# An edge stage of a graph network: the one-hot of an edge's rank is made by edge and turned a batch ahead

## The reference

```
k, q, v = typed_linear(x, ntype, Wk / Wq / Wv)
kw = rel_apply(k[src], etype, Watt);  m = rel_apply(v[src], etype, Wmsg)
a  = (kw * q[dst]).sum(-1) * pri[:, etype].T / sqrt(16)
ex = exp(a - segment_max(a, dst)[dst]);  alpha = ex / segment_sum(ex, dst)[dst]
agg = segment_sum(alpha[..., None] * m, dst)
out = silu(typed_linear(agg, ntype, Wa)) * al + x * (1 - al)   # al = sigmoid(skip[ntype])
x  = layernorm(out) * g + b
```

## Time and profile before

| | us |
|---|---|
| median of 3 runs | 3420.66 (3420.48 to 3424.94) |
| span of the profiled execution | 3418.8 |
| first gather of the first edge stage | 444.8 |
| first gather of the second edge stage | 1995.0 |
| last gather of the second edge stage | 3186.2 |

### The profile page before, as it was taken

One profiled execution on the slowest core, in us unless ns is written; L12 is line 12 of the kernel. 1 busy time (PEld: TensorE's weight loads), 2 busy tenths in 40 slices (PEclk: granted clock), 3 DMA queues, 4 the chain that ended last, 5 costly groups with the idle time before them and its releaser, 6 DMA issues. The chain is left out here.

```text
span 3418.8 us, 52858 instructions
## 1 busy us (share of the span) xinstructions
PE 2097.2 (61%) x12592; PEld 1812.6 (53%) x12592; DVE 2154.3 (63%) x5522; ACT 1534.9 (45%) x5149; POOL 1947.8 (57%) x2030
## 2 busy tenths in 40 slices
PE   2567726666666666666566626666666666666565
PEld 1455515556566555655444525556655555555544
DVE  6576527666666666666555626666666666666577
ACT  0015514444444444544555614444444444444554
POOL 4415555666666666666355564666666666666265
PEclk6568867776767777677677866776777767777655
DMA  5416655555555555555245554555555555555321
GB/s 125 80 74 262 274 159 143 152 154 157 154 153 153 154 155 151 156 154 152 71 188 200 218 161 141 148 153 155 152 155 155 154 157 156 153 153 151 111 56 31
DMA packets 386069, 511.26 MB, mean 150 GB/s; under 512 B 75321, under 2 KB 298235, under 8 KB 373268
## 3 DMA queue, kind: packets, MB, share of 16 engines
q0 software_dynamic: 101952, 326.75, 30.8%
q1 hardware_dynamic: 274712, 179.39, 17.9%
q10 hardware_dynamic: 9104, 1.86, 0.3%
HBM read 382.63 MB, written 142.96 MB: 154 GB/s over the span
## 5 line engine op out<-in xcount | busy, mean ns | idle before, releaser
L1242 POOL DMA_INDIRECT g_rows<-node_kv,edge_key_sb x1564 | 1478.4, 945 | 913.1 <-issue 415.8
L1412 ACT ACTIVATE acc<-g_ps_sum 128x127 f32 x1564 | 420.5, 269 | 691.9 <-issue 498.9
L1477 PE MATMUL g_ps_sum<-g_hot,g_rows 128*128 128x128 f32 x3128 | 597.1, 348 | 163.5 <-ACT acc L1416 118.0
L1496 PE MATMUL g_ps_q<-g_qw,g_hot_t 128*128 128x128 f32 x3128 | 629.6, 372 | 106.7 <-DVE g_rows L1268 43.5
L1416 ACT ACTIVATE acc<-acc,g_gained,g_scale x1564 | 601.1, 384 | 136.0 <-issue 120.5
L1477 PEld LDWEIGHTS g_ps_sum<-g_hot,g_rows 128*128 128x128 f32 x3128 | 545.1, 259 | 203.7 <-ACT acc L1416 138.2
L1496 PEld LDWEIGHTS g_ps_q<-g_qw,g_hot_t 128*128 128x128 f32 x3128 | 586.6, 282 | 119.5 <-issue 58.0
L1522 PE MATMUL g_ps_a<-g_ends,head_of_row 112*8 112x56 f32 x224 | 38.0, 270 | 551.9 <-DVE g_alpha L1303 461.9
L1485 PE MATMUL g_ps_hot<-ident,g_hot_t 128*128 128x128 f32 x1564 | 310.9, 325 | 50.6 <-issue 29.0
L1268 DVE TENSOR_TENSOR g_rows<-g_rows,g_ps_q 128x512 f32<-128x512 f32 (+1 forms) x446 | 263.3, 608 | 118.2 <-remote 85.2
L1522 PEld LDWEIGHTS g_ps_a<-g_ends,head_of_row 112*8 112x8 f32 x224 | 13.5, 88 | 576.1 <-issue 576.1
(11 more groups left out here) (247 smaller groups left out, 3204.1 us busy)
## 6 DMA issues: line engine op xcount, KB each, us to landing
g_qw<-node_q SPq DMA_DIRECT2D x1564, 64.0 KB
g_rank_row<-edge_rank SPq DMA_DIRECT2D x110, 448.0 KB
g_rows<-node_kv,edge_key_sb POOLq DMA_INDIRECT x1564
node_agg<-n_agg SPq DMA_DIRECT2D x24, 256.0 KB, 2.3
node_rows<-node_x SPq DMA_DIRECT2D x2, 1792.0 KB
node_q<-l_blank_q SPq DMA_DIRECT2D x1, 3200.0 KB
node_q<-n_q_sb,node_slot POOLq DMA_INDIRECT x112
node_kv<-n_kv,node_id POOLq DMA_INDIRECT x112
```

The costliest lines, as they stand in the source:

```text
L1242: g_.indirect_dma_start(out=rows[b % U][:, g, :], out_offset=None, in_=scratch["kv"][:, :], in_offset=bass.IndirectOffsetOnAxis(ap=tab["ke ...
L1412: a.activation(acc[:, bass.ds(w + 1, P - 1)], ps_sum[q % 2][:, n, 1:P], ACT.Copy).then_inc(s["copied"], 1)
L1477: ins = t.matmul(ps_sum[q % 2][:, n, :], rows[b % U][:, g, D:2 * D], hot[b % U][:, g, :], start=True, stop=True)
L1496: ins = t.matmul(ps_q[q % 2][:, n, :], hot_t[b % 2][:, g, :], qw[b % 2][:, g, :], start=True, stop=True)
```

## The change

The one-hot is now made with edges on the partitions: VectorE compares a row of numbers 0 to 127 in PSUM (`place_ps`, the same in every partition) with a column of ranks that stays in SBUF for the whole kernel (`tab["rank"]`, 128 x 784 bfloat16). The result is `hot` (four buffers, `HOT`), and `sums` reads it as it is. TensorE turns it a batch ahead, in step b the tiles of batch b + 1 (`following`), and ScalarE copies the turned tiles to a single `hot_t`, which `spread` reads; a copy waits until the spread of the same group of the batch before is done, a spread until its group is copied, and the first turn of a batch until its one-hot is made. The DMA of the row of ranks, its buffer and SP's wait are gone, and with them the tail of zeros in DRAM. In the step of TensorE groups 0 and 1 of the turn stand together behind sums(old, 1), in front of the ends matmul; in ScalarE's, turned(following, 0) stands behind means(old, 1). Before the first step TensorE turns and ScalarE copies batch 0. The stage of tables turns a fourth array, the ranks, and VectorE copies it in front of the counting loop.

```diff
@@ edge_tables
+                dve.wait_ge(s["pe"], 5)
+                did(v.tensor_copy(tiles_of(tab["rank"][:, :]), ps_t[1][:, 0:K7, 0:Q]))
                 dve.wait_ge(s["lows"], 1)
...
-                for i, a in enumerate((keyf, lo, hi)):
-                    pe.wait_ge(s["dv"], (7, 7, 14)[i])
+                for i, a in enumerate((keyf, lo, hi, rank)):
+                    pe.wait_ge(s["dv"], (7, 7, 14, 14)[i])
+                    if a is rank:
+                        pe.wait_ge(s["lows"], 1)
@@ edge_stage, SP
-                    if b + 1 < BATCHES:
-                        sp.wait_ge(s["hot_t"], b + 1)
-                        ranks(b + 1)
-
-                ranks(0)
@@ edge_stage, VectorE
                 def one_hot(b):
-                    n = SIZES[b]
-                    dve.wait_ge(ranks_in[b % 2], 16 * (b // 2 + 1))
-                    if b >= 2:
-                        dve.wait_ge(s["spread"], GROUP[b - 1])
-                        dve.wait_ge(s["turned_ps"], GROUP[b - 1])
-                    v.tensor_tensor(hot_t[b % 2][:, 0:n, :].rearrange("p g e -> p (g e)"), rank_row[:, 0:n * P], number_ps.to_broadcast([P, n * P]),
-                                    ALU.is_equal).then_inc(s["hot_t"], 1)
+                    at, n = FIRST[b], SIZES[b]
+                    if b >= HOT:
+                        dve.wait_ge(s["sums"], GROUP[b - HOT + 1])
+                    v.tensor_tensor(hot[b % HOT][:, 0:n, :], place_ps.rearrange("p (o r) -> p o r", o=1).to_broadcast([P, n, P]),
+                                    tab["rank"][:, at:at + n].rearrange("p (g o) -> p g o", o=1).to_broadcast([P, n, P]),
+                                    ALU.is_equal).then_inc(s["hot"], 1)
@@ edge_stage, ScalarE
                     act.wait_ge(s["turned_ps"], q + 1)
-                    a.activation(hot[b % U][:, four[0]:four[-1] + 1, :], ps_hot[q % 2][:, 0:len(four), :], ACT.Copy).then_inc(s["turned"], 1)
+                    if b >= 1:
+                        act.wait_ge(s["spread"], GROUP[b - 1] + k + 1)
+                    a.activation(hot_t[:, four[0]:four[-1] + 1, :], ps_hot[q % 2][:, 0:len(four), :], ACT.Copy).then_inc(s["turned"], 1)
...
                     if has(old, 0):
                         means(old, 0)
-                    if has(new, 0):
-                        turned(new, 0)
                     if has(old, 1):
                         means(old, 1)
+                    if has(following, 0):
+                        turned(following, 0)
@@ edge_stage, TensorE
                     if k == 0:
                         pe.wait_ge(s["message"], b + 1)
-                        pe.wait_ge(s["turned"], GROUP[b + 1])
...
                     if has(old, 0):
                         sums(old, 0)
-                    if has(new, 0):
-                        turn(new, 0)
                     if has(new, 2):
                         spread(new, 2)
                     if has(old, 1):
                         sums(old, 1)
-                    if has(new, 1):
-                        turn(new, 1)
+                    for k in range(2):
+                        if has(following, k):
+                            turn(following, k)
```

More of the change, by code:

```diff
@@ L1157, in edge_stage @@
     q_in = [s[f"q_in{u}"] for u in range(2)]
-    ranks_in = [s[f"ranks_in{u}"] for u in range(2)]
     EARLY = 8
+    HOT = 4
     with ExitStack() as st:
@@ L1164, in edge_stage @@
         qw = [sb(f"qw{u}", [P, G, D]) for u in range(2)]
-        rank_row = sb("rank_row", [P, G * P], BF16)
-        hot_t = [sb(f"hot_t{u}", [P, G, P]) for u in range(2)]
-        hot = [sb(f"hot{j}", [P, G, P]) for j in range(U)]
+        hot_t = sb("hot_t", [P, G, P])
+        hot = [sb(f"hot{j}", [P, G, P]) for j in range(HOT)]
         score = sb("score", [P, G, H])
@@ L1432, in step @@
                     new, mid, old = in_flight(b)
+                    following = b + 1 if b + 1 < BATCHES else None
                     has = lambda batch, k: batch is not None and k < len(FOURS[batch])
@@ L1456, in step @@
                         means(old, 3)
-                    if has(new, 3):
-                        turned(new, 3)
+                    if has(following, 3):
+                        turned(following, 3)
                     if new is not None:
                         flags(new)
+                for k in range(len(FOURS[0])):
+                    turned(0, k)
                 over(step, 2)
@@ L1476, in sums @@
                     for n, g in enumerate(FOURS[b][k]):
-                        ins = t.matmul(ps_sum[q % 2][:, n, :], rows[b % U][:, g, D:2 * D], hot[b % U][:, g, :], start=True, stop=True)
+                        ins = t.matmul(ps_sum[q % 2][:, n, :], rows[b % U][:, g, D:2 * D], hot[b % HOT][:, g, :], start=True, stop=True)
                     ins.then_inc(s["sums"], 1)
@@ L1481, in turn @@
                     q = GROUP[b] + k
+                    if k == 0:
+                        pe.wait_ge(s["hot"], b + 1)
                     if q >= 2:
@@ L1484, in turn @@
                     for n, g in enumerate(FOURS[b][k]):
-                        ins = t.transpose(ps_hot[q % 2][:, n, :], hot_t[b % 2][:, g, :], c["ident"][:, :])
+                        ins = t.transpose(ps_hot[q % 2][:, n, :], hot[b % HOT][:, g, :], c["ident"][:, :])
                     ins.then_inc(s["turned_ps"], 1)
@@ L1491, in spread @@
                         pe.wait_ge(q_in[b % 2], 16 * sum(SIZES[b % 2:b + 1:2]))
-                        pe.wait_ge(s["hot_t"], b + 1)
+                    pe.wait_ge(s["turned"], q + 1)
                     if q >= 2:
@@ L1495, in spread @@
                     for n, g in enumerate(FOURS[b][k]):
-                        ins = t.matmul(ps_q[q % 2][:, n, :], hot_t[b % 2][:, g, :], qw[b % 2][:, g, :], start=True, stop=True)
+                        ins = t.matmul(ps_q[q % 2][:, n, :], hot_t[:, g, :], qw[b % 2][:, g, :], start=True, stop=True)
                     ins.then_inc(s["spread"], 1)
@@ L1527, in step @@
                         sums(old, 2)
-                    if has(new, 2):
-                        turn(new, 2)
+                    if has(following, 2):
+                        turn(following, 2)
                     if has(old, 3):
                         sums(old, 3)
-                    if has(new, 3):
-                        turn(new, 3)
+                    if has(following, 3):
+                        turn(following, 3)
                     if mid is not None:
@@ L1536, in step @@
                         t.matmul(scale_ps[:, 0:2 * SIZES[mid]], c["head_of_feature"][:, :], share[:, :, 0:SIZES[mid]], start=True, stop=True).then_inc(s["scale_ps"], 1)
+                for k in range(len(FOURS[0])):
+                    turn(0, k)
                 over(step, 2)
@@ L1561, in gnn @@
         tab["pass"] = sb("tile_pass_sb", [H, T], BF16)
+        tab["rank"] = sb("edge_rank_sb", [P, T], BF16)
         unsorted = sb("unsorted", [1, 1], I32)
```

34 lines of the change are left out of this document (15 added, 19 removed).

## The result

The changed kernel takes **3463.8 us** (3461.1 to 3467.4, four runs), the kernel before 3422.8 (3420.5 to 3427.6, four runs): a ratio of 1.0117, interval 1.0102 to 1.0132. It is 41 us slower. The forecast was 3434, slower by 13; the measured time lies in the stated range and outside the forecast's own range of 3428 to 3442, just under the price of the rival "TensorE becomes the bound" (3466 to 3540, chance 0.21).

What follows compares the result with a forecast made beforehand. GpSimd's gather stream, pausing twice for late TensorE signals, was taken to set a 21.0 us batch. Span 3418.8 + 3.2 tables + 10 starts + 106 x 0 = 3432, plus 2 to the median: 3434 us; range 3385 to 3505.

Steps and rivals of the forecast that it cites:

- TensorE becomes the bound: Rival, chance 0.21: turned group 0's copy behind means(old, 1) makes the next first sums late; 3466 to 3540 us.
- What sets the pace: Edge stages: the gather stream delays TensorE's signals and sets its own pace, 21.0 us a batch; compute engines have slack.
- its sign of being wrong: Edge stages: the prediction called itself wrong if the batch is not 21.0 us long.
- The row of ranks at nothing: Edge stages: dropping the row's 112 DMAs was taken to gain 0, with 0.24 us a batch as the other end.
- the row held the gathers: Rival, chance 0.23: without the row the pause before gather 8 shrinks 0.24 us a batch, 25 us; 3409 or 3399.
- the slack grows: Rival, chance 0.04: TensorE's clock granted in full more often, first sums' signal earlier, the 1.65 us pause goes; 3259 us.
- The one-hot at 2.0 us: VectorE's one-hot from rank column and PSUM row: 2.0 us against today's 2010 ns, cost 0.
- They fit in: cost 0: TensorE: turn groups 0 and 1, waiting for the one-hot, fit its idle time before the ends matmul; cost 0.
- turns push out the ends matmul: Rival, chance 0.04: the ends matmul's signal then comes late, 2 us a batch or more; 3640 us.
- The chain that it gave: Copy of turned group 0 delays turn 2, scale matmul 1.1 us later, then next batch's first sums; decides from 0.8 us.
- Start of each edge stage: Batch 0's turn, copy and spread come first while gathers delay signals: 5 us a stage, 10 us in all.
- Stage of tables: VectorE's copy of the ranks stands in front of the counting loop: 3.2 us, ends 1.6 and 3.2.

Runs made afterwards that it cites:

- e11: The changed kernel unaltered, run again on a chip where the kernel before takes 2809.6 us: 2810.8 us, ratio 1.0003.
- e2: Changed kernel with a DMA of a row of ranks, which nothing reads, and its two waits put back: 3463.7 us, ratio 1.0132.
- e3: Kernel before with the row of ranks loaded only for batch 0, so part of the computation is left out: 3417.1 us, ratio 0.9992.
- e1: Changed kernel with turn groups 0 and 1 placed behind the ends matmul and the transpose of alpha: 3426.9 us, ratio 1.0012.
- e4: Changed kernel with ScalarE's copy of turned group 0 put back in front of means(old, 1): 3429.5 us, ratio 1.0025.
- e5: Changed kernel with one signal behind turn 1 counting for groups 0 and 1: 2810.6 us, where the kernel before takes 2809.3 us; ratio 1.0006.
- e7: Kernel before with turn groups 0 and 1 and ScalarE's copy of group 0 moved as in the changed kernel: 2814.4 us against 2809.3, ratio 1.0015.
- e10: Kernel before with turn groups 0 and 1 and ScalarE's copy of group 0 moved, run again on another chip: 2817.9 us against 2813.4, ratio 1.0019.
- e8: Changed kernel with turn groups 0 and 1 behind the ends matmul and the tables' rank copy on ScalarE: 2806.1 us against 2809.3, ratio 0.9992.

## Why the prediction was right or wrong

**What sets the pace: right, for 80 batches of 104.** The prediction read the two pauses as TensorE's signals arriving late while gathers stream. e11 bears it out: no late signal, no pause, and a batch of 17.5 us, which is the 14 gathers alone. But its sign of being wrong was a batch that is not 21.0 us long, and 24 batches are not (21.3 to 22.6).

**The row of ranks at nothing: right.** e2 and e3. The rival that the row held the gathers, at 0.24 us a batch, is out. So is "the slack grows": the clock in the window went from 0.73 to 0.75, and both pauses stayed.

**The one-hot at 2.0 us: right**, 2012 ns, and it starts at the same 1.56 us after gather 0 as before.

**"They fit in: cost 0", for turns 0 and 1 in front of the ends matmul: this is the step that failed.** The fit itself held: turns from 3.63 us, the ends matmul over at 6.28 in the median of both kernels. But the prediction costed TensorE's time and not its signals', though its first part says that these are late while gathers stream. In TensorE's order both turns stood in front of the ends matmul before, too, but they had mostly run some 4 us earlier (TensorE idle 4.52 us there); now both wait for the one-hot, and the second ends only 0.7 to 1.6 us before the end of the ends matmul, on which VectorE's second half depends. Held batches came of it, 47 for 6, and 36 us in all where 0 was put. The rival "turns push out the ends matmul" had the right place and the chance of 0.04; its own mechanism, a matmul issued later, did not occur, and its 2 us a batch came in 24 of 104 batches and as 1.28 us.

**"TensorE becomes the bound" (0.21)** had the right price and the right sign to look for: the second pause above 2.0 us with the first sums over less than 0.5 us before it. That is what the 24 batches show (0.27 us). The chain that it gave is not what makes them. In the batches that are not held the scale matmul is at 13.8 instead of 13.1 us, 0.7 later where 1.1 was forecast, and the first sums start at 17.5 as before; and in e1, where ScalarE's copy stays behind means(old, 1), the steady batches are only 4.4 us longer in all than before. What e4 gains is in the held batches, and there the copy's place does count, beside the turns' and not by itself. That the measured time lies in the stated range is therefore luck in good part: the range went up to 3505 for this rival, and the loss came by another way.

**Start of each edge stage, 2 x 5 us: wrong, it costs 0.3 and 1.7.** The last copies of batch 0 came through within 1 us (first edge stage, changed kernel):

```profile
464.13 3.35 PE L1483 MATMUL g_ps_hot<-ident,g_hot 128*128 128x128 f32 x14 [14.41 <-DVE g_hot L1248]
...
468.43 0.38 ACT L1415 ACTIVATE g_hot_t<-g_ps_hot 128x256 f32<-128x256 f32 x1 [0.74 <-PE g_ps_hot L1483]
...
517.33 2.02 DVE L1265 TENSOR_REDUCE g_score<-g_rows 128x112 f32<-128x1792 f32 x1
```

The reduction stands 61.7 us after the first gather, 61.8 before. In the second edge stage it is 3.4 us late (63.8 against 60.4), and 1.7 of that is left after three batches.

**Stage of tables, 3.2 us: right in its size**, but the first gather is 10.9 us late in this profile. The first hots start 2.8 us later; the rest is the counting loop, whose hots idle 57.7 us, before 46.8:

```profile
L571 DVE TENSOR_TENSOR e_hot_lo<-e_row_of,e_lo_t 128x1792 bf16<-128x1792 bf16 x56 | 61.3, 1094 | 57.7 <-remote 29.4 <-issue 18.4 <-PE e_ps_h L642 9.9
```
```profile
L571 DVE TENSOR_TENSOR e_hot_lo<-e_row_of,e_lo_t 128x1792 bf16<-128x1792 bf16 x56 | 61.1, 1092 | 46.8 <-remote 37.6 <-PE e_ps_h L640 9.2
```

The loop's length, from its first one-hot to the end of its last, changes from run to run with the same code: 130.9 us before, 128.5 in e3, 141.1 after, 133.4 in e1, 127.6 in e2, 129.3 in e4, and 92 us on the chips without late signals. So I take most of the 8 us for chance, which is not shown: the first gather comes at 446.2 to 455.7 us in the four profiles with the change (after, e1, e2, e4) and at 439.1 and 444.8 in the two without it (e3, before). On the other chips the change costs 2.3 to 5.5 us there.

So of the sum, 3.2 + 10 + 0 became about 3 + 2 + 36, if the rest of the tables' delay is chance.

**What stays open.** Why the ends matmul's signal is late with turns in front of it: their two signals, or something else about their place; e5 was made for it and met no chip that could tell. Why held batches are those with late second sums, and how ScalarE's copy acts on both (e4). What makes the two kinds of chip differ; no chip was seen in both, so it may also be a condition that changes with time. And why e7 and e10, the kernel before with moved turns, are 0.15% to 0.19% slower where nothing is held: the steady batches of e7 are as long as e8's (1821.1 against 1820.4 us in all), and 9 us lie behind the last gathers of the two edge stages, in a stretch that I did not follow.

## What to carry to other kernels

Work that fits into an idle stretch of an engine may still not be free if another engine waits for what that engine does next: here the matmul was as early as ever, and the engine that waited for it went on up to 5.5 us late. Put the instruction that somebody is waiting for ahead of work that nobody needs yet; that one move took the change from 1.2% slower to 0.1%. And a loss or gain of a per cent that comes from late signals can depend on the chip: run both kernels on more than one before deciding, since here it was 1.0117 on one kind and 1.0003 on the other.

## What the runs showed that I had not expected

The kernel before takes 3422 us on some chips and 2809 to 2813 on others. The changed kernel, of which there is a profile of each kind, has spans of 3465.6 and 2811.8 us, with VectorE's and GpSimd's durations the same (a gather 0.946 and 0.948 us). Most of the difference is idle time: in front of the 1564 gathers GpSimd idles 950.5 us on the one kind and 482.8 on the other, 468 of the 654 us. TensorE's busy time differs too, 2075.8 and 1875.3 us, at a mean granted clock of 0.75 and 0.81. ScalarE, whose L1408 waits in the code for nothing but signals that ScalarE itself gave (of the tile before), idles 114.8 us before it in the changed kernel and 5.2 in e11:

```profile
L1408 ACT ACTIVATE acc<-acc,g_gained,g_scale x1564 | 601.0, 384 | 114.8 <-issue 101.6 <-ACT acc L1404 11.1
```
```profile
L1408 ACT ACTIVATE acc<-acc,g_gained,g_scale x1564 | 601.7, 385 | 5.2 <-issue 3.8
```

So even a signal from ScalarE to itself seems to be late there. The Trainium skill ("VectorE: DVE Perf Modes", section "The TRN2 errata — SBUF-src ops pay a fixed extra latency per instruction") warns that dense signals at the end of instructions, from several engines, should be spaced, because of a deadlock. No run here shows a deadlock, nor signals spaced evenly; but e1, in which the turns' two signals no longer stand ahead of the ends matmul's, has no held batch.
